# Householder columns of an eigenvector kernel: no unread streams on TensorE while two tiles are left, and the layer norm pieces moved up in ScalarE's column

## The reference

```python
# layer 0: eight Euler steps of a graph ODE, then a layer norm
h = einsum('bnd,ed->bne', x, fc_in_w) + fc_in_b
for _ in range(8):
    ax = einsum('nm,bmd->bnd', adj, h)
    h = h + (alph * 0.5 * (ax - h) + h @ w_eff - h + x) / 8
x = layernorm(x + h)
# layer 1: spectral network in the eigenvectors of the normalised Laplacian
_, U = eigh(L_norm(adj))                 # 512 x 512
out = relu(einsum('mn,bnd->bmd', U.T, x) @ W1 + b1) @ W2 + b2
x = layernorm(x + einsum('nm,bmd->bnd', U, out))
```

## Time and profile before

| | us |
|---|---|
| median of 3 runs | 4076.65 |
| the profiled execution's own time | 4106.44 |
| its span | 4104.0 |
| columns 0 to 126 (four tiles), 27 to 904 | 877 |
| columns 127 to 254 (three tiles), 904 to 1635.6 | 731.6 |
| columns 255 to 282 (two tiles, with Euler units), 1635.6 to 1788 | 152.4 |
| columns 283 to 382 (two tiles, streams only), 1788 to 2333.5 | 545.5 |
| columns 383 to 510 (one tile), 2333.5 to 2833.7 | 500.2 |
| divide and conquer and spectral network, 2833.7 to 4104 | 1270.3 |

### The profile page before, as it was taken

One profiled execution on the slowest core, in us unless ns is written; L12 is line 12 of the kernel. 1 busy time (PEld: TensorE's weight loads), 2 busy tenths in 40 slices (PEclk: granted clock), 3 DMA queues, 4 the chain that ended last, 5 costly groups with the idle time before them and its releaser, 6 DMA issues.

```text
span 4104.0 us, 62250 instructions
## 1 busy us (share of the span) xinstructions
PE 2870.3 (70%) x13748; PEld 2207.5 (54%) x13749; DVE 3388.4 (83%) x19331; ACT 1096.1 (27%) x4884; POOL 847.6 (21%) x4216
## 2 busy tenths in 40 slices
PE   7999999999999999899888866665013322121078
PEld 6677677776767767668667666664013311010033
DVE  7887999999888888776887777777888998989924
ACT  2322333333333333333444333332000000000013
POOL 3241222222222222222222333332000000000000
PEclk9887999999999999775888755555556666565589
DMA  2000000000000000000000000000000000000001
GB/s 62 1 1 1 1 1 1 1 1 1 1 1 2 1 1 1 1 6 1 1 1 1 1 1 1 1 1 26 0 1 0 1 1 0 0 0 0 0 0 41
DMA packets 14584, 17.39 MB, mean 4 GB/s; under 512 B 1664, under 2 KB 11008, under 8 KB 13952
## 3 DMA queue, kind: packets, MB, share of 16 engines
q1 hardware_dynamic: 14208, 13.42, 1.1%
HBM read 9.22 MB, written 4.19 MB: 3 GB/s over the span
## 4 chain that ended last, share of the span: by engine, by line
DVE 51%; PE 37%; issue 6%; POOL 3%; ACT 3%; DMA 0%; DVEq 0%; POOLq 0%
PE ps L684 7%; PE ps L723 6%; DVE h L2078 4%; PE ps L777 3%; PE ps L710 2%; PE ps L654 2%; PE ps L640 2%; DVE ps L1575 2%; PE ps L702 2%; DVE am L1488 2%; DVE small L1589 2%; PE ps L662 2%; DVE junk L1562 2%; DVE eye L1562 2%; DVE small L1573 2%
## 5 line engine op out<-in xcount | busy, mean ns | idle before, releaser
L684 PE MATMUL ps<-ident 128*128 128x256 f32 x2992 | 874.5, 434 | 0.0
L684 PEld LDWEIGHTS ps<-ident 128*128 128x128 f32 x2992 | 597.8, 214 | 77.6 <-issue 7.0
L723 PEld LDWEIGHTS ps<-UR 128*128 128x128 f32 x2552 | 390.3, 217 | 188.5 <-DVE UR L1646 93.3
L723 PE MATMUL ps<-UR 128*128 128x41 f32 (+17 forms) x2552 | 397.9, 288 | 93.1 <-ACT UR L1280 69.9
L1068 POOL TENSOR_SCALAR small<-small 128x1 f32<-128x1 f32 x511 | 118.4, 232 | 1296.3 <-ACT small L1244 1278.3
L777 PEld LDWEIGHTS ps<-small,ones 128*128 128x128 f32 x766 | 132.2, 209 | 321.8 <-DVE am L1610 302.3
L702 PE MATMUL ps<-UR,ident 128*128 128x18 f32 (+2 forms) x1020 | 239.6, 318 | 89.4 <-DVE UR L1577 89.4
L1264 ACT ACTIVATE small<-lower,small 128x1 f32<-128x1 f32 x383 | 112.9, 295 | 669.9 <-DVE small L1593 669.9
L1242 ACT ACTIVATE small<-ps 128x1 f32<-128x1 f32 x511 | 87.6, 171 | 760.7 <-PE ps L723 760.7
L777 PE MATMUL ps<-small,ones 128*128 128x2 f32 x766 | 152.5, 269 | 160.6 <-DVE am L1610 159.5
L702 PEld LDWEIGHTS ps<-UR,ident 128*128 128x128 f32 x1020 | 195.0, 239 | 100.4 <-DVE UR L1577 100.4
(11 more groups left out here) (621 smaller groups left out, 7600.8 us busy)
## 6 DMA issues: line engine op xcount, KB each, us to landing
out<-xs SPq DMA_DIRECT2D x16, 256.0 KB, 2.3
m<-in_adj SPq DMA_DIRECT2D x1, 1024.0 KB, 5.8
before<-c_before SPq DMA_DIRECT2D x1, 1024.0 KB, 4.7
notafter<-c_notafter SPq DMA_DIRECT2D x1, 1024.0 KB, 8.2
sib<-c_sib SPq DMA_DIRECT2D x1, 448.0 KB, 3.0
own<-c_own SPq DMA_DIRECT2D x1, 384.0 KB, 4.9
iota<-c_iota SPq DMA_DIRECT2D x1, 256.0 KB, 2.7
h<-c_lanes SPq DMA_DIRECT2D x1, 186.0 KB, 2.4
```

The lines of the kernel that those rows point to most:

```text
L684: nc.tensor.matmul(ps[1][:, 0:2 * P].rearrange("p (a d) -> p a d", a=2), ident[:, 0:P], ident[:, 0:P].unsqueeze(1).broadcast_to([P, 2, P]) ...
L723: last = nc.tensor.matmul(ps[2][:, 0:2 * npend + 3], over(x_of(j)), flat[:, j, 2 * first:2 * k + 3], start=(j == tp), stop=(j == T - 1))
```

## The change

Two edits. The first sets the streams of columns 283 to 382 to none: the rule for columns in which the units have run out now ends in zero streams when two tiles are left. The second moves ScalarE's norm piece from the end of the column to the place behind the copies of the norms (L1244) and the units that stand there; this holds for all columns that take a piece, those with one tile left as well. Nothing is added, and no result that is read changes.

```diff
             if k >= 8 and left < sum(wanted):
                 units, extra = (0, left, 0), (2 * wanted[0], 2 * wanted[1] + extra[1] - 2 * left, 2 * wanted[2])
                 extra = tuple(max(0, e) for e in extra)
+                if n_on == 2:
+                    extra = (0, 0, 0)
             units_of.append(units)
             halves_of.append(extra)
@@ ScalarE's column
                     nc.scalar.activation(NA[:, 2:5], ps[2][:, 0:3], ACT.Copy).then_inc(root_ready, 1)
                 for _ in range(euler_units(k)[0]):
                     next(state, None)
+                if takes_norm(k):
+                    next(norms)
                 if n_on > 1 and product_by_tensor(k):
@@
                 for _ in range(euler_units(k)[1]):
                     next(state, None)
-                if takes_norm(k):
-                    next(norms)
                 stage = panel_stage(k)
```

## The result

Over 20 runs of each the changed kernel took 4093.85 us in the median (4077.68 to 4111.56), the kernel before 4066.85 us (4043.60 to 4103.76). The ratio is 1.0069, with a 95% interval of [1.0050, 1.0089]. The forecast was 4087 us, a change of 10 us; the change measured 27 us. Two copies of one and the same kernel differed by 0.23% (experiment 3), so 0.7% is a small effect but a real one.

The account below looks back on a forecast made before the run. It took the columns as a loop of latencies at full clock, TensorE-bound at half clock. 100 x 5.37 + 3 gives 540 us against an assumed 530 in the median: 10 us more than 4076.65, so 4087; range 4045 to 4120.

Parts of the forecast that it names:

- The clock without streams: Columns 283 to 382: TensorE at 1.2 GHz for all 100 columns once their streams are gone.
- The first rival: Columns 283 to 382: clock stays full without streams, 4.68 us a column, 471 us with panels, 4031 or 4018 total; 5%.
- A column at 1.2 GHz: Two-tile column without streams: column 342 goes from 4.61 to 5.24 us; a mean column takes 5.37.
- 3 us for panels: First part of the sum's extras: 0.25 us for two columns in each of 6 panels.
- The moved pieces: ScalarE's norm pieces: moving them gains or loses nothing in one-tile columns, and 0.06 us in two-tile columns at full clock.
- the 0.06 us a column: Two-tile columns at full clock: time by which L1238, behind the norm piece, held L723.
- I take half: the median execution had 530 us here: Columns 283 to 382: half the profiled run's 30 us excess assumed here, so the change makes the median 10 us longer.
- The second rival: Columns 283 to 382: median lacks the half-clock piece, part 506, change 34 more, 4111; 25%, plus 10% beyond 1% slower.
- the long piece at half clock: Columns 291 to 308 of the profiled execution: 18 columns at 1.2 GHz in one piece, costing 39 us.

Follow-up runs that it names:

- experiment 3: Kernel before run again unchanged, twice, for further traces; the second copy had a median of 4083.23 us, ratio 1.0023 against the kernel before.
- kernel 5: Norm pieces moved, two streams ahead of cy and none behind the pivot row in columns 283 to 382; 4111.88 us against 4071.87 for the kernel before.
- kernel 6: Norm pieces moved, two streams ahead of cy and two behind the pivot row in columns 283 to 382; 4184.80 us against 4071.87 for the kernel before.
- third trace of before: Unchanged kernel before, traced a third time; execution 4059.22 us, columns 283 to 382 in 499.5 us.
- second trace: Unchanged kernel before, traced a second time; execution 4110.05 us, columns 283 to 382 in the same 545 us as in the first trace.

## Why the prediction came out as it did

- **The clock without streams:** right. 1.2 GHz for all 100 columns, read off the one-tile columns. The first rival, that it holds, is refuted by this trace and by kernel 5, which had even two streams a column and a clock of 0.50. What the Trainium skill, "TensorE: Matmul & The Clock Gate", says under "What's actually happening", that activity releases the throttle, agrees with these runs only in part: with five streams in every column the clock was 0.99, with none 0.50, but kernel 6 was busy in 212.31 us of a stretch of 212.40 and stayed at 0.50. The same page of the Trainium skill blames, in its section "HAM oscillation", idle waits between bursts; in kernel 6 there were hardly any, and in column 342 of the changed kernel, at 0.50 too, the longest was 1.79 us.
- **A column at 1.2 GHz:** right, step by step. In the line numbers of the changed kernel, the forecast had L1644 at 2.80 (2.78 measured), the next vector L1654 at 3.06 (3.04), L1490 at 3.24 (3.22), the end of L1518 at 4.07 (4.07), the dots L725 at 4.14 (4.14 for their load, 4.17 for their matmuls), 1.07 for the dots (1.01) and the column at 5.24 (5.22). The mean was 5.37 and 3 us for panels, 540 in all; the part measured 538.3, in columns of 5.19 to 5.75.
- **The moved pieces:** right for the one-tile columns and for the changed kernel, where they are worth nothing. The prediction counts 28 pieces in columns 383 to 420; `takes_norm` gives 38, which changes nothing, since each costs nothing. For a kernel that keeps its streams the 0.06 us a column was right and the worth of the edit was not foreseen: 26 us, with a clock of 0.93 in the part.
- **The term that was mis-sized:** "I take half: the median execution had 530 us here". By the estimate of experiment 3 it had 502 to 511. The profiled execution's excess over the median, which the runs of before put at 30 us and the 20 runs at 40, lay in this part nearly whole: 545.5 less 502 to 511 is some 35 to 43. With 502 to 511 in the place of 530 the same working gives a change of 29 to 38 us, against the 27 measured. The second rival, that the long piece at half clock is missing in a median execution (506 us, and 34 us more), was the nearer one, and had 25%. It holds in the third trace of before, where no long piece occurs, three panels lose the clock for a few columns each, and the part is 499.5; in the second trace there is such a piece, in columns 321 to 340.
- **Luck:** the forecast time of 4087 us lies only 7 below the 4093.85 measured, but two errors cancel in it. The change was 17 us too small, and the 4076.65 that it was added to, the median of three runs, was 10 us above the median of 20.

So the mechanism and the price of the new state were right, and the size of the old state was not. Three runs and one trace of a long execution don't give it.

## What to carry to other kernels

Where a filler is there to hold a clock, there are three prices: with enough of it, with none, and with too little. Here the worst was one piece too little (four streams where five hold the clock), since it was paid at the low clock and bought next to nothing; two streams in the gap cost only 14 us, in the panels. So look for the places where the filler is one piece short (the panels here) before taking it out. A part whose time depends on the clock has to be read in several executions before a difference of traces is worth anything; the medians of variants whose part is fixed give an estimate for the one whose part is not, as far as the rest of the kernel is alike.

## What the runs showed of the hardware that was not expected

- How steeply the clock answers to one stream. Each figure is from one traced execution, but for the five streams, with three. In two-tile columns the mean clock was 0.99 with five streams a column and 0.53 with four; in one-tile columns 1.00 with four and 0.71 with three. The kernel before stood between, with five in most columns and four in the panels', at 0.78, 0.78 and 0.91 in three executions, and that is where its spread of 60 us comes from in large part.
- At 1.2 GHz a TensorE that is busy without a pause stayed there for long: over the 126 us of the earlier trace rows, and in kernel 6 for the 212 us shown, and, but for a return in columns 321 to 324 and a shorter one at 353, for the rest of the 629 us. Both lie in a panel's columns or just behind them. Busy is meant as the view counts it, from the start of a record to an end that is modelled, so short pauses may be hidden in it. Being busy in this sense did not by itself bring 2.4 GHz back in that time; what ended such a stretch was not found.
